# Graph network layer on one core: clearing ahead of every seventh gather, a fifth TensorE tile, one release per chunk

## The chip, the cores and the metric

The kernel runs on one core of a Trainium2 chip. The metric is the device time of one execution in microseconds, lower is better. TensorE (PE in the profile) multiplies matrices and writes PSUM; VectorE (DVE), ScalarE (ACT) and GpSimd (POOL) work on SBUF and PSUM; SyncE (SP) issues most DMAs. Each engine has its own instruction stream, and the streams meet only at semaphores.

## The reference

One layer of message passing over a graph of 6250 nodes with 64 features and 206,250 edges, sorted by destination (`dst`):

```python
h = jnp.maximum(_layernorm(x, axis=-1), 0.0)
msg = jax.nn.relu(h[src] + edge_attr)
agg = jax.ops.segment_sum(msg, dst, num_segments=x.shape[0])
z = jax.nn.relu((h + agg) @ W1 + b1)
out = x + (z @ W2 + b2)
```

## The kernel before, in words

The edges are cut into 124 chunks of 13 tiles with 128 edges each. Four chunks make a turn; there are 31 turns. Turn 0 is written out, turns 1 to 27 are a loop on every engine, and turns 28 to 30 (`EARLY_TURNS`) are written out again, since the two dense layers of the nodes that are already complete run beside them. Chunk number u of a turn has its own buffers (`gath[u]`, `onehot[u]`, `ends[u]`).

The rows `h[src]` of a chunk come in two ways. For most tiles GpSimd issues an indirect DMA per tile (`gather_rows`, L360), which fetches 128 rows of `h_table` from HBM. For the others TensorE picks the rows itself: `h` lies in SBUF as a high and a low float16 part (`table_hi`, `table_lo`); a one-hot of the source's block (`keyhot`) is multiplied with both, in seven blocks, so 14 matmuls of 448 columns per tile (`candidates`, L1083). The result holds seven candidate rows per edge in a PSUM bank of `ps_cand`; VectorE multiplies it with a mask (L842) and reduces it (L848) to the row that is wanted. `PE_TILES` says how many tiles of each chunk of a turn go this way: 4, 4, 4, 4, so that GpSimd gathers 9 per chunk.

VectorE adds the edge attributes to the gathered rows (L878, `sum_edges`), applies the ReLU and splits each partition's 13 edges by whether they belong to its first or its last destination (L888, `part_edges`, two instructions), reduces the parts over the 13 edges (L898, `add_parts`), and makes a one-hot of the destinations (L860). In the loop the edge attributes are copied by ScalarE into PSUM (L625, `edge_near`), and the sum and the parts read them there. TensorE multiplies `ends` with the one-hot (L384, `scatter_ends`), which adds the messages of a node up in a window of 64 nodes, and VectorE adds the window to `agg` (L919).

No planner sets the order; it is the order in which the code is written for each engine. Around the change these waits matter:

- GpSimd's gathers of chunk c wait for the chunk's indices, for the sum of the chunk four back (`summed`), which frees the buffer, and at four places in the chunk for TensorE to have finished one tile each of the chunk two back (`cands_ready`, the `released` argument, L358). The last kind protects no data; it sets the pace of the gathers.
- TensorE's tiles wait for a bank of `ps_cand` to be read (`masked`, four banks), and a chunk waits for its `keyhot`, two blocks of which VectorE makes and five ScalarE.
- VectorE's sum waits for the chunk's gathers (`gathered[u]`) and for its own last reduction.
- SyncE loads keys, indices and edges for two chunks at a time (`load_pair`).

## Time and profile before

| | us |
|---|---|
| three runs | 1792.00, 1792.09, 1795.76 (median 1792.09) |
| profiled execution, its own time | 1784.28 |
| its span | 1782.5 |
| TensorE busy | 1503.6 (84%) |
| VectorE busy | 1400.8 (79%) |
| GpSimd busy | 1107.6 (62%) |
| ScalarE busy | 793.4 (45%) |
| mean granted TensorE clock, share of full speed | 0.918 |

The span runs from the first to the last instruction; the rest of the execution's own time lies around it. Busy shares are averages over the start, the loop and the end. Matmuls are pipelined, so that the mean duration of one, as the page gives it, overlaps the next one. "issue" as a releaser means that an engine waited for nothing that the profile shows; "remote" is a releaser that the profile can't place.

### The profile page before, as it was taken

What the parts mean: (1) busy time and instruction counts of PE and PEld (TensorE: products, weight loads), DVE (VectorE), ACT (ScalarE), POOL (GpSimd) and SP (SyncE); (2) the same over time, 40 slices, a digit from 0 to 9 for tenths busy, and PEclk for the clock granted to TensorE, in tenths of its full rate; (3) what the DMA queues carried; (4) which work ended last, traced back from release to release, by engine and by line L of the source; (5) the groups of instructions that cost most, each with busy time, mean ns of one, the idle gap of its engine ahead of it and who ended that gap; (6) DMA issues with size and microseconds to landing.
All of it is one profiled execution on the core that took longest, in us unless ns stands there. A gap on an engine that the chain in (4) does not pass through costs nothing.

```text
span 1782.5 us, 26009 instructions
## 1 busy us (share of the span) xinstructions
PE 1503.6 (84%) x7987; PEld 729.3 (41%) x7987; DVE 1400.8 (79%) x2068; ACT 793.4 (45%) x883; POOL 1107.6 (62%) x1139
## 2 busy tenths in 40 slices
PE   5597898889888899888988888988889889898775
PEld 3243344434444444444434434434444444443432
DVE  8587788878887887878878878777888788798565
ACT  5244444544544544444445444544454445453321
POOL 5776566666666666656666666566666666567660
PEclk9798899999999999989989999989999999998896
DMA  4312122222222222221222222212222222222120
GB/s 165 94 45 73 46 73 72 48 72 72 47 73 71 47 73 53 67 72 47 72 67 52 72 57 63 71 47 73 72 47 73 68 51 73 66 53 73 45 60 20
DMA packets 67162, 115.15 MB, mean 65 GB/s; under 512 B 29810, under 2 KB 32882, under 8 KB 67010
## 3 DMA queue, kind: packets, MB, share of 16 engines
q1 hardware_dynamic: 30130, 75.86, 13.1%
q0 software_dynamic: 36000, 36.94, 11.3%
q10 hardware_dynamic: 1008, 2.06, 0.3%
q8 instruction: 12, 0.20, 0.0%
q14 instruction: 12, 0.10, 0.0%
HBM read 111.43 MB, written 3.34 MB: 64 GB/s over the span
## 4 chain that ended last, share of the span: by engine, by line
PE 77%; issue 13%; DVE 6%; POOL 1%; another core or an unknown queue 1%; DMA 0%; DVEq 0%; ACT 0%; ACTq 0%
PE ps_cand L1083 74%; PE ps L384 2%; DVE parts L888 2%; POOL gath L360 1%; DVE picked L842 1%; DVE gath L848 1%; PE ps_edge L413 1%; DVE ends L898 1%; PE ps_edge L428 1%; DMA xh<-x_rows 0%; DVE xh L751 0%; DVE row_ssq L742 0%; DVEq L909 0%; DVE side L796 0%
## 5 line engine op out<-in xcount | busy, mean ns | idle before, releaser
L360 POOL DMA_INDIRECT gath<-h_table,idx_pair x1125 | 1100.1, 978 | 629.3 <-issue 317.1
L1083 PE MATMUL ps_cand<-table_hi,keyhot 128*128 128x448 f16 x3388 | 1247.9, 368 | 80.6 <-issue 76.9
L1083 PE MATMUL ps_cand<-table_lo,keyhot 128*128 128x448 f16 x3388 | 1246.7, 368 | 69.8 <-issue 68.5
L1083 PEld LDWEIGHTS ps_cand<-table_hi,keyhot 128*128 128x128 f16 x3388 | 342.4, 101 | 450.4 <-issue 169.6
L842 DVE TENSOR_TENSOR picked<-ps_cand,cand_mask 128x448 f32<-128x448 f32 x487 | 300.8, 618 | 277.7 <-remote 170.4
L1083 PEld LDWEIGHTS ps_cand<-table_lo,keyhot 128*128 128x128 f16 x3388 | 342.3, 101 | 424.4 <-issue 151.4
L634 ACT ACTIVATE keyhot<-key_pair,key_bias 128x512 f16<-128x512 f16 (+2 forms) x600 | 375.4, 701 | 161.8 <-remote 93.0
L625 ACT ACTIVATE ps_edge<-edge_pair 128x832 f32<-128x832 f32 x108 | 93.7, 868 | 663.7 <-DVE parts L888 442.9
L888 DVE SCALAR_TENSOR_TENSOR parts<-ps_edge,side 128x832 f32<-128x832 f32 x216 | 326.2, 1587 | 1.7 <-issue 1.7
L848 DVE TENSOR_REDUCE gath<-picked 128x64 f32<-128x448 f32 x487 | 296.3, 608 | 4.1
L638 ACT ACTIVATE keyhot<-keyhot,hot_bias 128x2560 f16<-128x2560 f16 (+2 forms) x120 | 287.2, 2393 | 3.9
L898 DVE TENSOR_REDUCE ends<-parts 128x128 f32<-128x1664 f32 x124 | 232.4, 1874 | 0.0
L878 DVE TENSOR_TENSOR ps_edge<-gath,ps_edge 128x832 f32<-128x832 f32 x108 | 110.0, 1019 | 0.0
L384 PE MATMUL ps<-onehot,ends 128*32 128x64 f32 x992 | 49.4, 236 | 69.1 <-issue 68.1
L727 DVE TENSOR_SCALAR keyhot<-key_pair,key_iota 128x512 f16<-128x512 f16 (+2 forms) x268 | 82.4, 352 | 0.5 <-issue 0.3
L384 PEld LDWEIGHTS ps<-onehot,ends 128*32 128x32 f32 x992 | 26.8, 112 | 105.4 <-issue 104.2
L919 DVE TENSOR_TENSOR agg<-agg,ps 128x64 f32 x124 | 27.4, 221 | 53.1 <-DVE agg L919 25.9
L419 ACT ACTIVATE xh<-ps_edge,b_sb 64x448 f32<-64x448 f32 (+2 forms) x14 | 8.8, 628 | 106.3 <-PE ps_edge L413 91.3
L860 DVE TENSOR_TENSOR onehot<-iota_f,place 128x128 f32<-128x128 f32 x124 | 35.0, 282 | 20.8 <-remote 20.8
L413 PE MATMUL ps_edge<-agg,w_sb 128*64 128x448 f32 (+2 forms) x28 | 18.0, 738 | 36.6 <-DVE agg L919 13.9
L888 DVE SCALAR_TENSOR_TENSOR parts<-xh,side 128x832 f32<-128x832 f32 x32 | 48.4, 1591 | 0.0
L618 ACT ACTIVATE agg<-ps 64x512 f32<-64x512 f32 (+1 forms) x8 | 7.3, 995 | 38.5 <-remote 29.1
(77 smaller groups left out, 161.3 us busy)
## 6 DMA issues: line engine op xcount, KB each, us to landing
edge_pair<-edges_t SPq DMA_DIRECT2D x62, 832.0 KB
gath<-h_table,idx_pair POOLq DMA_INDIRECT x1125
key_pair<-key_table SPq DMA_DIRECT2D x62, 256.0 KB
h_table<-xh SPq DMA_DIRECT2D x7, 224.0 KB, 2.4
x_b<-x_cols SPq DMA_DIRECT2D x1, 1568.0 KB
out<-x_sq SPq DMA_DIRECT2D x6, 224.0 KB
idx_pair<-src_t SPq DMA_DIRECT2D x62, 13.0 KB
xh<-x_rows ACTq DMA_DIRECT2D x4, 224.0 KB, 5.0
```

The source lines that it names most:

```text
L360: nc.gpsimd.indirect_dma_start(out=gath[u][:, r, :], out_offset=None, in_=h_table, in_offset=bass.IndirectOffsetOnAxis(ap=idx[u][:, r:r + ...
L384: last = nc.tensor.matmul(bank[k * D + d:k * D + d + QUARTER, 0:WIN], ends[u][:, k, d:d + QUARTER], onehot[u][:, k, :], start=True, stop=True)
L625: nc.scalar.activation(edge_near, edge[u], ACT.Copy).then_inc(edge_copied, 1)
L634: last = nc.scalar.activation(keyhot[u % 2][:, a, 0:n], key[u][:, P * PE_MAX - n:], ACT.Abs, bias=key_bias[:, a:a + 1])
L638: nc.scalar.activation(keyhot[u % 2][:, DVE_BLOCKS:, 0:n], keyhot[u % 2][:, DVE_BLOCKS:, 0:n], ACT.Relu, bias=hot_bias[:, 0:1], scale=-1.0 ...
L727: last = nc.vector.tensor_scalar(keyhot[u % 2][:, a, 0:n], key[u][:, P * PE_MAX - n:], key_iota[:, a:a + 1], 1.0 / SCALE, ALU.is_equal, AL ...
L842: nc.vector.tensor_tensor(picked[i][:, :, :], ps_cand[buf][:, 0:D * CAND].rearrange("p (d b) -> p d b", b=CAND), mask.to_broadcast([P, D, ...
L848: nc.vector.tensor_reduce(gath[u][:, pool_tiles(t, u) + i, :], picked[i][:, :, :], AX_X, ALU.add).then_inc(selected, 1)
L878: nc.vector.tensor_tensor(edge_near if near(t) else edge_sum, gath[u][:, :, :], edge_near if near(t) else edge[u], ALU.add).then_inc(summe ...
L888: last = nc.vector.scalar_tensor_tensor(out=parts[:, k, :, :].rearrange("p d r -> p r d"), in0=edge_near if near(t) else edge_sum, scalar=0.0,
L898: nc.vector.tensor_reduce(ends[u][:, :, :], parts[:, :, :, :], AX_X, ALU.add).then_inc(ends_ready, 1)
L1083: last = nc.tensor.matmul(bank[:, 0:D * CAND], keyhot[u % 2][:, a, i * P:(i + 1) * P], half[:, a, :, :].rearrange("p d b -> p (d b)"), sta ...
```

## The change

- `rest` is new: GpSimd clears a scratch area of 128x832 float32 (`rest_area`), which nothing reads, ahead of every seventh gather in the loop. It waits for the clearing before it. In turn 0 and in the last three turns there is none.
- `PE_TILES` becomes 4, 5, 4, 4: in one chunk of a turn of the loop TensorE picks five tiles and GpSimd gathers eight. `place_bank` gives the 17 tiles of a turn their banks of `ps_cand`. Buffers of keys, masks and one-hots grow from 4 places to 5; turn 0 and the last three turns keep their tiles.
- `gather_chunk` waits for TensorE once per chunk, for the first tile of the chunk two back, in place of four times.
- SyncE loads the first two pairs of edges at the start, ahead of the key table's store and of `h_table`, in place of behind them.
- `scatter_ends` takes 64 columns of weights at once in place of two times 32.
- `part_edges` writes `parts` in order and reads the sums with a stride of 64 elements; before it read them in order and wrote with a stride.
- The input for the residual (`x_b`) is loaded in two pieces, behind the first and the second sum; the weights are loaded without a wait.

```diff
--- before.py
+++ after.py
...
@@ -57,6 +56,7 @@
 LAST_ROWS = 3
+X_PIECES = 2
 PARTS = [range(g * GROUP, (g + 1) * GROUP) for g in range(EARLY_GROUPS)] + \
...
@@ -73,16 +73,18 @@
-PE_TILES = (4, 4, 4, 4)
+PE_TILES = (4, 5, 4, 4)
 PE_FIRST = (3, 4, 4, 4)
 PE_LAST = ((4, 4, 4, 4), (3, 4, 3, 4), (3, 3, 2, 2))
 PE_MAX = max(PE_TILES)
 PE_TURN = sum(PE_TILES)
-assert PE_FIRST[-1] == PE_TILES[-1] and PE_MAX == max(*PE_FIRST, *PE_LAST[0], *PE_LAST[1], *PE_LAST[2])
+assert PE_FIRST[-1] == PE_TILES[-1] and PE_MAX >= max(*PE_FIRST, *PE_LAST[0], *PE_LAST[1], *PE_LAST[2])
 CAND = GROUP
 KEY_BLOCKS = N_GROUPS
 DVE_BLOCKS = 2
+REST_AFTER = 7
+REST_COLS = 832
 CAND_BANKS = 4
...
@@ -120,12 +122,17 @@
+def place_bank(place):
+    whole = PE_TURN // CAND_BANKS * CAND_BANKS
+    return place % CAND_BANKS if place < whole else (place - whole + CAND_BANKS // 2) % CAND_BANKS
+
+
 def cand_bank(t, u, i):
     if isinstance(t, int) and t == 0:
-        return (sum(PE_FIRST[:u]) + i + PE_TURN - sum(PE_FIRST)) % CAND_BANKS
+        return place_bank(sum(PE_FIRST[:u]) + i + PE_TURN - sum(PE_FIRST))
     if isinstance(t, int) and t in EARLY_TURNS:
         return (pe_before(t, u, i) - pe_before(EARLY_TURNS[0], 0)) % CAND_BANKS
-    return (sum(PE_TILES[:u]) + i) % CAND_BANKS
+    return place_bank(sum(PE_TILES[:u]) + i)
...
@@ -136,10 +143,10 @@
     place = sum(PE_TILES[:u]) + i
-    same = [q for q in range(place) if q % CAND_BANKS == place % CAND_BANKS]
+    same = [q for q in range(place) if place_bank(q) == place_bank(place)]
     if same:
         return pe_before(t, 0, same[-1] + 1)
-    return pe_before(t, 0, [q for q in range(PE_TURN) if q % CAND_BANKS == place % CAND_BANKS][-1] + 1 - PE_TURN)
+    return pe_before(t, 0, [q for q in range(PE_TURN) if place_bank(q) == place_bank(place)][-1] + 1 - PE_TURN)
...
@@ -351,12 +360,21 @@
-        def gather_rows(u, tiles, signal, released=None):
+        def rest(count):
+
+            if count is not None:
+                nc.gpsimd.wait_ge(rested, count)
+                nc.gpsimd.sem_inc(slot_taken, 1)
+            nc.gpsimd.memset(rest_area[:, :], 0.0).then_inc(rested, 1)
+
+        def gather_rows(u, tiles, signal, released=None, rests={}):
             for r in range(tiles):
-                if released is not None and r in released:
-                    nc.gpsimd.wait_ge(cands_ready, released[r])
+                if released is not None and r == 0:
+                    nc.gpsimd.wait_ge(cands_ready, released)
                     nc.gpsimd.sem_inc(slot_taken, 1)
+                if r in rests:
+                    rest(rests[r])
                 nc.gpsimd.indirect_dma_start(
...
@@ -380,9 +398,8 @@
             for k in range(ENDS):
-                for d in range(0, D, QUARTER):
-                    last = nc.tensor.matmul(bank[k * D + d:k * D + d + QUARTER, 0:WIN],
-                                            ends[u][:, k, d:d + QUARTER], onehot[u][:, k, :], start=True, stop=True)
+                last = nc.tensor.matmul(bank[k * D:(k + 1) * D, 0:WIN], ends[u][:, k, :], onehot[u][:, k, :],
+                                        start=True, stop=True)
             last.then_inc(signal, 1)
...
@@ -452,6 +469,9 @@
                 sp.dma_start(idx_pair[h][:, :, :], src_t[:, h * PAIR:(h + 1) * PAIR, :]).then_inc(idx_loaded[h], 16)
+            for h in range(PAIRS):
+                sp.dma_start(edge_pair[h][:, :, :, :], edges_t[:, h * PAIR:(h + 1) * PAIR, :, :]
+                             ).then_inc(edge_loaded[h], 16)
...
@@ -465,9 +485,6 @@
                              ).then_inc(h_stored, 16)
-            for h in range(PAIRS):
-                sp.dma_start(edge_pair[h][:, :, :, :], edges_t[:, h * PAIR:(h + 1) * PAIR, :, :]
-                             ).then_inc(edge_loaded[h], 16)
             def load_pair(t, h):
...
@@ -486,13 +503,15 @@
-            sp.wait_ge(summed, 1)
             sp.dma_start(b1_sb[:, :], b1).then_inc(weights_loaded, 16)
             for half in range(2):
                 sp.dma_start(w1_sb[half * D:(half + 1) * D, :], w1).then_inc(weights_loaded, 16)
             sp.dma_start(w2_sb[0:D, :], w2).then_inc(weights_loaded, 16)
             sp.dma_start(w2_sb[D:D + 1, :], b2).then_inc(weights_loaded, 16)
-            sp.dma_start(x_b[:, :, :], x_cols).then_inc(weights_loaded, 16)
+            for k in range(X_PIECES):
+                rows = slice(k * NODES_PER_PART // X_PIECES, (k + 1) * NODES_PER_PART // X_PIECES)
+                sp.wait_ge(summed, k + 1)
+                sp.dma_start(x_b[:, rows, :], x_cols[:, rows, :]).then_inc(weights_loaded, 16)
...
@@ -544,9 +563,13 @@
                 old_t, old_u = back(t, u, 2)
-                n, m = pool_tiles(t, u), pe_tiles(old_t, old_u)
-                gather_rows(u, n, gathered[u], {i * n // m: pe_before(old_t, old_u, i) + 1 for i in range(m)})
-
+                before = sum(pool_tiles(1, k) for k in range(u))
+                rests = {r: (before + r) // REST_AFTER for r in range(pool_tiles(1, u)) if (before + r) % REST_AFTER == 0}
+                turn_rests = sum(pool_tiles(1, k) for k in range(SLOTS)) // REST_AFTER
+                gather_rows(u, pool_tiles(t, u), gathered[u], pe_before(old_t, old_u) + 1,
+                            {} if isinstance(t, int) else {r: t * turn_rests + (n + 1 - turn_rests) for r, n in rests.items()})
+
+            pool.sem_inc(rested, 1)
             with pool.Fori(1, EARLY_TURNS[0]) as t:
...
@@ -886,10 +909,10 @@
                     last = nc.vector.scalar_tensor_tensor(
-                        out=parts[:, k, :, :].rearrange("p d r -> p r d"), in0=edge_near if near(t) else edge_sum,
+                        out=parts[:, k, :, :], in0=(edge_near if near(t) else edge_sum).rearrange("p r d -> p d r"),
                         scalar=0.0,
-                        in1=side[:, bass.ds(t * SLOTS + u, 1), k, :].rearrange("p c r -> p (c r)").unsqueeze(2)
-                        .to_broadcast([P, TILES_PER_CHUNK, D]), op0=ALU.max, op1=ALU.mult)
+                        in1=side[:, bass.ds(t * SLOTS + u, 1), k, :].rearrange("p c r -> p (c r)").unsqueeze(1)
+                        .to_broadcast([P, D, TILES_PER_CHUNK]), op0=ALU.max, op1=ALU.mult)
                 last.then_inc(parted, 1)
...
```

What moves on GpSimd, in the loop's body from its start (line 544, now 563, waits for indices; 358, now 374 and 366, are register work of waits; 360, now 378, is the gather). Before:

```order
14 L544 ISA
15 L358 ISA
16 L360 DMA gath<-h_table,idx_pair 128x64 x2
17 L358 REGISTER_ALU
18 L360 DMA gath<-h_table,idx_pair 128x64 x2
19 L358 REGISTER_ALU
20 L360 DMA gath<-h_table,idx_pair 128x64 x2
21 L358 REGISTER_ALU
22 L360 DMA gath<-h_table,idx_pair 128x64 x3
```

And of the changed kernel, the same place, the first chunk and the beginning of the second:

```order
14 L563 ISA
15 L374 ISA
16 L366 ISA
17 L368 MEMSET rest_area 128x832
18 L378 DMA gath<-h_table,idx_pair 128x64 x7
19 L366 REGISTER_ALU
20 L368 MEMSET rest_area 128x832
21 L378 DMA gath<-h_table,idx_pair 128x64 x2
22 L563 REGISTER_ALU
23 L374 REGISTER_ALU
24 L378 DMA gath<-h_table,idx_pair 128x64 x5
25 L366 REGISTER_ALU
```

The nine gathers of a chunk stood in four groups, each behind a wait for TensorE; now they stand in runs of seven across the chunks, with a clearing between the runs.

What moves on TensorE, at the two scatters that follow the second chunk of a turn (L384, now L401). Before:

```order
361 L384 MATMUL ps<-onehot,ends 32x64 [waits ends_ready,accumulated]
362 L384 MATMUL ps<-onehot,ends 32x64 x3
363 L1091 REGISTER_ALU
364 L384 MATMUL ps<-onehot,ends 32x64 [waits ends_ready,accumulated,onehot_ready]
365 L384 MATMUL ps<-onehot,ends 32x64 x3
```

And of the changed kernel:

```order
376 L401 MATMUL ps<-onehot,ends 64x64 [waits ends_ready,accumulated]
377 L401 MATMUL ps<-onehot,ends 64x64
378 L1114 REGISTER_ALU
379 L401 MATMUL ps<-onehot,ends 64x64 [waits ends_ready,accumulated,onehot_ready]
380 L401 MATMUL ps<-onehot,ends 64x64
```

The scatters stand at the same place with the same waits, 14 matmuls of the fifth tile later, and have half as many matmuls.

## Rows read from the trace of the kernel before

**Rows 1.** The page, parts 1 and 4: busy us, share, instructions; shares of the last chain
```profile
PE 1503.6 (84%) x7987; PEld 729.3 (41%) x7987; DVE 1400.8 (79%) x2068; ACT 793.4 (45%) x883; POOL 1107.6 (62%) x1139
PE 77%; issue 13%; DVE 6%; POOL 1%; another core or an unknown queue 1%; DMA 0%; DVEq 0%; ACT 0%; ACTq 0%
```

**Rows 2.** The page, part 5: groups of instructions; busy us, mean ns, idle before
```profile
L360 POOL DMA_INDIRECT gath<-h_table,idx_pair x1125 | 1100.1, 978 | 629.3 <-issue 317.1
L1083 PE MATMUL ps_cand<-table_hi,keyhot 128*128 128x448 f16 x3388 | 1247.9, 368 | 80.6 <-issue 76.9
L842 DVE TENSOR_TENSOR picked<-ps_cand,cand_mask 128x448 f32<-128x448 f32 x487 | 300.8, 618 | 277.7 <-remote 170.4
L848 DVE TENSOR_REDUCE gath<-picked 128x64 f32<-128x448 f32 x487 | 296.3, 608 | 4.1
L888 DVE SCALAR_TENSOR_TENSOR parts<-ps_edge,side 128x832 f32<-128x832 f32 x216 | 326.2, 1587 | 1.7 <-issue 1.7
L878 DVE TENSOR_TENSOR ps_edge<-gath,ps_edge 128x832 f32<-128x832 f32 x108 | 110.0, 1019 | 0.0
```

**Rows 3.** Timeline of VectorE: one-hots of chunks, and its wait between two of them
```profile
118.22 0.28 DVE L860 TENSOR_TENSOR onehot<-iota_f,place 128x128 f32<-128x128 f32 x1
901.72 0.29 DVE L860 TENSOR_TENSOR onehot<-iota_f,place 128x128 f32<-128x128 f32 x1 [6.96 <-remote]
919.18 0.62 DVE L842 TENSOR_TENSOR picked<-ps_cand,cand_mask 128x448 f32<-128x448 f32 x1 [2.38 <-PE ps_cand L1083]
927.13 0.28 DVE L860 TENSOR_TENSOR onehot<-iota_f,place 128x128 f32<-128x128 f32 x1
1592.95 0.28 DVE L860 TENSOR_TENSOR onehot<-iota_f,place 128x128 f32<-128x128 f32 x1
```

**Rows 4.** Windows: us, busy time of each engine (instructions), granted clock, DMA share, GB/s
```profile
578.00:589.00 11.00, 11.00 (x59) 5.56 (x57) 10.37 (x15) 6.39 (x7) 8.20 (x9) 1.00 0.20 46
589.00:593.30 4.30, 0.82 (x8) 0.39 (x7) 3.45 (x4) 0.87 (x1) 1.89 (x2) 0.94 0.11 23
1227.00:1248.00 21.00, 21.00 (x102) 10.43 (x101) 15.30 (x26) 11.04 (x12) 13.13 (x15) 0.90 0.28 76
62.00:100.00 38.00, 19.24 (x56) 5.09 (x57) 10.72 (x18) 7.80 (x9) 25.71 (x25) 0.55 0.16 34
150.00:1590.00 1440.00, 1260.68 (x6777) 613.34 (x6776) 1161.87 (x1690) 678.92 (x740) 902.20 (x952) 0.94 0.25 63
```

**Rows 5.** Timelines of GpSimd, then TensorE: start, us, instruction, idle before and releaser
```profile
589.09 0.94 POOL L360 DMA_INDIRECT gath<-h_table,idx_pair  x1 [0.46 <-issue]
590.34 0.95 POOL L360 DMA_INDIRECT gath<-h_table,idx_pair  x1 [0.30 <-issue]
617.01 0.94 POOL L360 DMA_INDIRECT gath<-h_table,idx_pair  x1 [1.17 <-remote]
156.66 0.31 PE L384 MATMUL ps<-onehot,ends 128*32 128x64 f32 x3 [0.71 <-issue]
1575.00 0.34 PE L384 MATMUL ps<-onehot,ends 128*32 128x64 f32 x5 [1.11 <-issue]
```

**Rows 6.** Waits, whole span: engine, line, releaser; us in total, times, longest
```profile
PEld ps_cand L1083 <- issue: 321.0, 661, 3.4
POOL gath L360 <- PE ps_cand L1083: 138.0, 84, 5.4
```

**Rows 7.** Groups by shape, GpSimd and VectorE
```profile
L526 POOL IOTA iota_p<- 128x1 int32 x1 | 0.1, 119 | 0.0
L525 POOL IOTA iota_i<- 128x128 int32 x1 | 0.2, 236 | 0.4 <-POOLq L1207 0.4
L399 POOL TENSOR_TENSOR xh<-xh,row_mean 128x448 f32<-128x448 f32 x7 | 6.9, 1013 | 4.7 <-ACT row_mean L579 4.7
L772 DVE SCALAR_TENSOR_TENSOR table_lo<-xh,table_hi 128x448 f16<-128x448 f32 x7 | 5.9, 934 | 0.0
```

**Rows 8.** Timeline of GpSimd: its first gather
```profile
22.79 6.09 POOL L360 DMA_INDIRECT gath<-h_table,idx_pair  x1 [10.03 <-DMA h_table<-xh]
```

9 lines of the change are left out of this document (5 added, 4 removed).

## The prediction

> **What bounds the kernel now.** I read the page's busy shares and its chain first. TensorE is busy for 84% of the span, and the chain that ended last runs through it for 77% and through "issue" for 13%, time in which an engine waited for nothing that the profile shows [rows 1]. So TensorE carries the end, and part of it is lost to something that isn't a semaphore. The costliest groups [rows 2] give the work of a turn of the loop. A turn is four chunks and takes 54.6 us: the one-hot of the first chunk of turn 1 starts at 118.22 and that of turn 28 at 1592.95, 27 turns later [rows 3].
>
> What each engine needs for a turn, if nothing waits:
> - TensorE: in a calm stretch 59 matmuls start in 11.00 us [rows 4], 0.186 us each. A tile has 14 of them, 2.61 us; 16 tiles are 41.8 us, with the scatters about 43.
> - VectorE: from the one-hot at 901.72 to the one two chunks later at 927.13 it waits once, 2.38 us [rows 3]. Two chunks are 25.41 - 2.38 = 23.0 us, a turn 46.1.
> - GpSimd: gathers that don't wait start 1.25 us apart (589.09 and 590.34), 0.94 of work and 0.30 behind it [rows 5]. 36 of them are 45.0 us.
>
> None reaches 54.6. The waits show where the rest is: the weight load stands idle for 321 us by "issue", 661 times [rows 6]. I walked through TensorE's and GpSimd's timelines from 150 to 1590 us and put together TensorE's idle spells of at least 0.4 us that lie under 3 us apart: 57 stretches, 139 spells, 150 us, the first spell ending at 156.66, the last at 1575.00 [rows 5]. Beside each I counted the gathers that GpSimd had issued without a pause. 54 of the 57 begin at the 8th to 11th gather of such a run, one at the 7th, and two right behind a run of nine and a pause of 1.17 us (the gather at 617.01 [rows 5]). None begins in a run of six or fewer. The windows show it from both sides [rows 4]: nine gathers and a full TensorE up to 589.00, then 0.82 us of matmuls in 4.30 us; 25 gathers without a pause and 19 of 38 us at a granted clock of 0.55 in the first turn; and in 1227 to 1248 fifteen gathers, broken by short pauses, with TensorE busy for 21.00 of 21.00 us. I can't name what TensorE lacks in a stretch; that long gather runs bring it on is as plain as a trace can make it.
>
> The price now: 150 us / 26.4 turns = 5.7 us of idle a turn. The clock falls from its upper to its lower level (2.4 to 1.2 GHz) behind such idle: 0.94 over 1440 us [rows 4] is 12% of the time at half speed, 173 us, of which half is lost, 3.3 us a turn. 43 + 5.7 + 3.3 = 52; the remaining 2.6 are short spells and waits on VectorE.
>
> One rule of the Trainium skill speaks against this reading. "Runtime: NRT & Kernel Launch", section Instruction fetch mechanics, puts fetch stalls at taken branches whose target isn't held, which no pause on GpSimd would touch. This case's trace doesn't agree: the stretch at 589 starts ahead of the loop's branch, and the one behind the gather at 617.01 [rows 5], half a turn later, lies in the middle of the body.
>
> **The change, part by part.** Times below are for a turn of the loop; 27 turns have the change, the first turn and the last three have no clearing.
> - A clearing of 128x832 float32 ahead of every seventh gather, five a turn. The trace has no such instruction. The nearest rows [rows 7]: an iota of one column 0.119 us and one of 128 columns 0.236, so 0.92 ns per further column and 0.88 us for 832; a subtraction with two inputs 1.013 us for 448, 2.26 ns per column, 1.88 us. Bounds: 0.12 us, if width costs nothing, and 1.9; I take 0.88, since the iota too only writes. With one more 0.30 us behind it a rest adds 1.18 us, five add 5.9.
> - 35 gathers in place of 36: 43.75 us. GpSimd's turn is 43.75 + 5.9 = 49.6 us (45.9 to 54.7 between the bounds).
> - A fifth tile on TensorE in one chunk: 14 x 0.186 = 2.6, so 44.4 and with the scatters, whose matmuls are half as many, about 45. VectorE gains a product (0.618) and a reduction (0.608) [rows 2] that overlap by a tenth: 46.1 + 1.2 = 47.3.
> - VectorE writes the parts in order and reads the sums with a stride, before the other way. Before: 1.587 us for 832 against 1.019 for the sum of the same size [rows 2], so the strided side costs 0.57. A strided read is in the trace only from SBUF: 0.934 for 448 columns [rows 7] against the 0.618 of VectorE's product of 448 in order [rows 2], 0.7 ns per column, which for 832 is again 0.57 to 0.59. So I take no gain. The lower bound, that a strided read of PSUM costs nothing, would give VectorE 8 x 0.57 = 4.5 us a turn. Either way VectorE (42.8 to 47.3) stays below GpSimd's 49.6, and the sum doesn't move.
> - One release per chunk in place of four. A release is a wait of GpSimd on TensorE; 138 us in 84 waits have TensorE as their last releaser [rows 6], and they are what breaks the gather runs now. If they go, nothing but the clearing breaks them. Behind the waiting instruction are the gathers of the chunk, and VectorE's sum waits for those. With GpSimd as the slowest engine the one wait left is mostly met when it is reached; I add 1.0 us a turn for it and for the waits on loaded indices.
> - Edges ahead of keys: two transfers of 832 KB are issued some 17 us earlier, ahead of the key table's. They are done before the first sum needs them now too; nothing gained, up to 2 us lost if the keys land later. The residual's input in two pieces, its second behind another sum: used only in the last turns, nothing. Wider masks and keys (5 places for 4) make the first turn's masks and key work about 2 us longer.
> - The last three turns keep their tiles, with one release for four and no clearing: runs of nine and more. They take stalls now and will then; I put nothing, with 8 us to either side.
>
> The rest decides whether the stretches go. A cycle is 7 gathers and a rest, 9.9 us, 1.42 us per gather. The stretch from 1227 to 1248 had 1.40 us per gather, broken as finely, and no stall [rows 4]. I take it that they go, and with them the low clock: TensorE then has 45 us of work in a turn of 50 and short idle spells only.
>
> Sum: a turn becomes 49.6 + 1.0 = 50.6 us, 4.0 less; 27 turns give -108; the start +2. The profiled execution took 1784.3 us by its own time (span 1782.5, 1.8 around it), so 1678; the runs' median, 1792.1, is 7.8 above that execution, so 1686.
>
> The skill has a price for the clearing that no row has: "GPSIMD Engine Reference", section 3.1, gives a one-input loop at best 769 ns for 512 elements. By it, as an estimate, the clearing is 1.25 us, GpSimd's turn 51.5, and the whole about 1737 - no run here shows it yet.
>
> **The rivals.**
> 1. Part of the stalls stays. The pause of 1.17 us at 617 did not stop the stretch behind a run of nine [rows 5], and 1.42 us per gather, kept up for a whole turn, is denser than the 54.6 / 36 = 1.52 of now. If half of the 9.0 us of stall and low clock stays, TensorE's turn is 45 + 4.5 + 2.6 = 52.1, 1784.3 - 67 + 10, about 1727; if the clearing costs 1.9 us as the subtraction would, GpSimd's 54.7 gives today's time, 1792. Range 1718 to 1792. Chance 0.19, of which 0.04 ends within 0.2% of now.
> 2. The clearing is cheap and enough. At its lower bound GpSimd needs 45.9, and VectorE's 47.3 is the bound (or TensorE's 45, if the parts get faster): 27 x 7.3 = 197 less, about 1597; with part of the waits kept, up to 1645. For it: nothing shows how little GpSimd must leave free. Against it: it takes a one-column price for 832. Chance 0.07.
> 3. Slower. GpSimd's clearing doesn't count as a pause: the stretches come as before, since what disturbs TensorE goes on while GpSimd is busy with anything, and the fewer releases lengthen the runs. Its place is TensorE's stream in the loop; its price is the fifth tile on a bound engine, 27 x 2.6 = 70, so 1862, and more if runs lengthen. It decides when the clearing saves less than 2.6 of the 9.0 us a turn. For it: every pause in the trace is idleness, none is work of GpSimd. A harsher form: the first gather behind other GpSimd work took 6.09 us [rows 8]; if every switch cost that, the turn would gain 26 us. Against that: it came once, and the gathers behind it took 0.94. Chance 0.14.
>
> **How the numbers follow.** Forecast (1645 to 1718): 0.60. A difference under 0.2%, some 3.6 us, can't be told from none. Faster: 0.60 + 0.15 + 0.07 = 0.82; same 0.04; slower 0.14. The range reaches from 1640, a little into rival 2, to 1790, through rival 1: outside are about 0.04 below and 0.14 above.
>
> **What would show it.** Right: the weight load's idle by "issue" falls from 321 us to under 120, what is left sits in the first turn and the last three; the granted clock from 150 us on is above 0.97; GpSimd has no wait over 1 us in the loop and a turn of 50 to 51; clearing near 0.9 us. VectorE's parts at 1.6 us (1.0 would say that PSUM's stride is free). Wrong: stretches of issue idle in the loop behind seven gathers and a clearing; gathers over 2 us behind a clearing; a turn at or above 54.6.

## The result and the profile after

The changed kernel takes 1891.95 us (1883.06 to 1896.21, 4 runs) beside 1793.24 for the kernel before (1792.0 to 1795.76): ratio 1.0535, 95% interval 1.0514 to 1.0557. It is 5.3% slower; 1686 was forecast.

The page of the profiled execution, its parts 1 and 4 as in [rows 1]: busy time and share of each engine, then the engines' shares of the chain that ended last.

```profile
PE 1516.7 (80%) x7869; PEld 758.4 (40%) x7869; DVE 1353.0 (72%) x2122; ACT 824.4 (44%) x883; POOL 1187.5 (63%) x1247
...
PE 67%; DVE 11%; another core or an unknown queue 11%; issue 9%; DVEq 1%; DMA 1%; ACTq 0%; ACT 0%
```

The chain goes less through TensorE and "issue" than before, and 11% of it now runs through a releaser that the profile can't place. Part 5 (busy us, mean ns, idle before and its releaser), to be read against [rows 2]:

```profile
L378 POOL DMA_INDIRECT gath<-h_table,idx_pair x1098 | 1071.4, 976 | 602.7 <-issue 297.4
L1106 PE MATMUL ps_cand<-table_hi,keyhot 128*128 128x448 f16 x3577 | 1306.3, 365 | 282.2 <-DVE picked L865 230.4
...
L865 DVE TENSOR_TENSOR picked<-ps_cand,cand_mask 128x448 f32<-128x448 f32 x514 | 317.2, 617 | 472.9 <-remote 330.8
...
L911 DVE SCALAR_TENSOR_TENSOR parts<-ps_edge,side 128x832 f32<-128x832 f32 x216 | 210.0, 1013 | 0.0
L368 POOL MEMSET rest_area<- 128x832 f32 x135 | 108.7, 805 | 50.2 <-PE ps_cand L1106 48.1
```

None of these instructions became slower, and the parts fell from 1587 to 1013 ns. (Those that make the wider keys of the fifth tile did, ScalarE's from 701 to 725 ns on the mean.) What grew is waiting: TensorE 80.6 to 282.2 us ahead of the matmuls with `table_hi` (150 to 295 us with those of `table_lo`), VectorE 277.7 to 472.9 ahead of its picks (the product at L865). The view of the waits (us in total, times, longest), against [rows 6]:

```profile
DVE picked L865 <- remote: 330.8, 82, 19.1
...
POOL gath L378 <- PE ps_cand L1106: 283.2, 61, 18.8
PEld ps_cand L1106 <- DVE picked L865: 241.4, 25, 15.4
PE ps_cand L1106 <- DVE picked L865: 230.4, 23, 14.9
PEld ps_cand L1106 <- issue: 166.6, 407, 13.6
...
POOL rest_area L368 <- PE ps_cand L1106: 48.1, 24, 2.1
```

And two more lines of the same view of the kernel before:

```profile
POOL gath L360 <- remote: 164.1, 64, 5.2
...
PE ps_cand L1083 <- DVE picked L842: 2.4, 4, 1.3
```

The weight load's idle by "issue" fell from 321.0 to 166.6 us, as hoped. GpSimd's waits by name of TensorE seem to double, from 138.0 to 283.2, but before, 164.1 us more of them stood under "remote". The releases are counted one by one below. TensorE's wait on a pick now comes 23 times with 10 us each, where before it came 4 times with 2.4 us in all. The loop's turn, from the one-hot of turn 1 to that of turn 28, as in [rows 3]:

```profile
123.35 0.28 DVE L883 TENSOR_TENSOR onehot<-iota_f,place 128x128 f32<-128x128 f32 x1
...
1693.07 0.28 DVE L883 TENSOR_TENSOR onehot<-iota_f,place 128x128 f32<-128x128 f32 x1
```

58.1 us in place of 54.6: 27 x 3.5 = 95 of the 110 us by which the span is longer (1892.2 against 1782.5). The rest is what lies ahead of turn 1 (+5) and the last three turns (+10). The window of [rows 4] shows the clock at 0.91 against 0.94:

```profile
150.00:1590.00 1440.00, 1207.19 (x6345) 606.24 (x6345) 1052.69 (x1652) 671.49 (x700) 922.76 (x992) 0.91 0.22 60
```

What happens in a turn, in the timelines of GpSimd, VectorE and TensorE (start, us, instruction, idle before and releaser):

```profile
957.13 0.96 POOL L378 DMA_INDIRECT gath<-h_table,idx_pair  x1 [0.30 <-issue]
...
957.62 0.35 PE L1106 MATMUL ps_cand<-table_lo,keyhot 128*128 128x448 f16 x1
...
958.09 0.81 POOL L368 MEMSET rest_area<- 128x832 f32 x1
...
959.06 1.07 POOL L378 DMA_INDIRECT gath<-h_table,idx_pair  x1 [0.17 <-issue]
...
960.27 0.35 PE L1106 MATMUL ps_cand<-table_lo,keyhot 128*128 128x448 f16 x1
...
962.83 0.61 DVE L871 TENSOR_REDUCE gath<-picked 128x64 f32<-128x448 f32 x1
...
966.87 0.94 POOL L378 DMA_INDIRECT gath<-h_table,idx_pair  x1 [0.30 <-issue]
967.80 0.82 POOL L368 MEMSET rest_area<- 128x832 f32 x1
968.78 0.95 POOL L378 DMA_INDIRECT gath<-h_table,idx_pair  x1 [0.17 <-issue]
969.84 0.62 DVE L865 TENSOR_TENSOR picked<-ps_cand,cand_mask 128x448 f32<-128x448 f32 x1 [6.40 <-remote]
...
970.52 0.55 PE L1106 MATMUL ps_cand<-table_hi,keyhot 128*128 128x448 f16 x1 [9.90 <-DVE picked L865]
```

The tile that the pick at 969.84 reads was finished by the matmul at 957.62, which ended at 957.97. VectorE was free from 963.44. The pick starts 6.4 us later, 2.0 us behind the end of a gather run (967.81), when a clearing has passed and the next gather is already at work. What was late is neither work nor an engine but TensorE's signal. TensorE meanwhile did one more tile, to 960.62, and then needed the bank that this pick frees: 9.9 us lost. GpSimd, a few gathers later, waits for TensorE in its turn. The three wait in a circle, and a pick over 5 us late comes 23 times from 160 to 1500 us, about once a turn.

GpSimd's own waits show the same without VectorE. I put beside each of its releases (the waits on TensorE's tiles) the end of the tile that it waits for, from 160 to 1450 us:

| kernel | releases | waits over 0.6 us | of them for a tile already done | their median |
|---|---|---|---|---|
| before | 378 | 103 | 100 | 2.6 us |
| changed | 89 | 67 | 44 | 2.1 us |

So also in the kernel before nearly every wait at a release is no wait for TensorE's work. The tile is done, GpSimd has stopped issuing gathers, and the signal arrives mostly 2 to 3 us after the last of them. Such pauses, four or so a turn, are when TensorE's signals catch up. In the changed kernel there are three a turn, and the 23 that aren't for a done tile are the far side of the circle: they end 0.79 us after a tile that TensorE finished late. One row of the 44:

```profile
948.69 0.79 POOL L368 MEMSET rest_area<- 128x832 f32 x1 [1.99 <-PE ps_cand L1106]
```

Added up, these waits give the turn. In the kernel before they cost GpSimd 9.1 us a turn beyond the usual 0.30 between gathers; with 36 x 1.25 = 45.0 of work that is 54.1 of the 54.6 measured. In the changed kernel they cost 10.4; with 47.1 of work (35 gathers and five clearings of 0.67, see the second sitting) that is 57.5 of 58.1. So three of four releases went, and none of the waiting did.

### The profile page after: what moved, and what is told of

Read it like the earlier page. It is cut to its first block, busy times and chain, and to the rows that moved or that the text cites. A ratio compares the mean times of both kernels' runs of the same rounds, so it can differ in the third digit from the quotient of the medians.

```text
span 1892.2 us, 25606 instructions
## 1 busy us (share of the span) xinstructions
PE 1516.7 (80%) x7869; PEld 758.4 (40%) x7869; DVE 1353.0 (72%) x2122; ACT 824.4 (44%) x883; POOL 1187.5 (63%) x1247
## 4 chain that ended last, share of the span: by engine, by line
PE 67%; DVE 11%; another core or an unknown queue 11%; issue 9%; DVEq 1%; DMA 1%; ACTq 0%; ACT 0%
PE ps_cand L1106 64%; DVE parts L911 3%; DVE picked L865 3%; DVE gath L871 3%; PE ps L401 1%; DVE ends L921 1%; PE ps_edge L430 1%; PE ps_cand L1080 1%; DVE keyhot L750 0%; DVEq L865 0%; PE ps_edge L445 0%; DMA xh<-x_rows 0%; DVE ps_edge L901 0%; DMA key_table<-key_h 0%
## 5 line engine op out<-in xcount | busy, mean ns | idle before, releaser
L1106 PE MATMUL ps_cand<-table_hi,keyhot 128*128 128x448 f16 x3577 | 1306.3, 365 | 282.2 <-DVE picked L865 230.4
L378 POOL DMA_INDIRECT gath<-h_table,idx_pair x1098 | 1071.4, 976 | 602.7 <-issue 297.4
L1106 PE MATMUL ps_cand<-table_lo,keyhot 128*128 128x448 f16 x3577 | 1302.0, 364 | 12.4 <-issue 12.2
L865 DVE TENSOR_TENSOR picked<-ps_cand,cand_mask 128x448 f32<-128x448 f32 x514 | 317.2, 617 | 472.9 <-remote 330.8
L1106 PEld LDWEIGHTS ps_cand<-table_hi,keyhot 128*128 128x128 f16 x3577 | 359.6, 101 | 652.5 <-DVE picked L865 241.4
L871 DVE TENSOR_REDUCE gath<-picked 128x64 f32<-128x448 f32 x514 | 314.5, 612 | 5.1
L911 DVE SCALAR_TENSOR_TENSOR parts<-ps_edge,side 128x832 f32<-128x832 f32 x216 | 210.0, 1013 | 0.0
L368 POOL MEMSET rest_area<- 128x832 f32 x135 | 108.7, 805 | 50.2 <-PE ps_cand L1106 48.1
L750 DVE TENSOR_SCALAR keyhot<-key_pair,key_iota 128x512 f16<-128x512 f16 (+3 forms) x268 | 107.0, 443 | 1.9 <-DMA key_pair<-key_table 1.5
L430 PE MATMUL ps_edge<-agg,w_sb 128*64 128x448 f32 (+2 forms) x28 | 19.5, 787 | 48.4 <-DVE x_sq L455 24.6
L911 DVE SCALAR_TENSOR_TENSOR parts<-xh,side 128x832 f32<-128x832 f32 x32 | 49.6, 1590 | 0.0
L401 PE MATMUL ps<-onehot,ends 128*64 128x64 f32 x496 | 31.3, 238 | 7.9 <-issue 6.8
L401 PEld LDWEIGHTS ps<-onehot,ends 128*64 128x64 f32 x496 | 21.4, 139 | 34.8 <-issue 33.7
```

Source lines behind the costliest of these rows:

```text
L368: nc.gpsimd.memset(rest_area[:, :], 0.0).then_inc(rested, 1)
L378: nc.gpsimd.indirect_dma_start(out=gath[u][:, r, :], out_offset=None, in_=h_table, in_offset=bass.IndirectOffsetOnAxis(ap=idx[u][:, r:r + ...
L750: last = nc.vector.tensor_scalar(keyhot[u % 2][:, a, 0:n], key[u][:, P * PE_MAX - n:], key_iota[:, a:a + 1], 1.0 / SCALE, ALU.is_equal, AL ...
L865: nc.vector.tensor_tensor(picked[i][:, :, :], ps_cand[buf][:, 0:D * CAND].rearrange("p (d b) -> p d b", b=CAND), mask.to_broadcast([P, D, ...
L871: nc.vector.tensor_reduce(gath[u][:, pool_tiles(t, u) + i, :], picked[i][:, :, :], AX_X, ALU.add).then_inc(selected, 1)
L911: last = nc.vector.scalar_tensor_tensor(out=parts[:, k, :, :], in0=(edge_near if near(t) else edge_sum).rearrange("p r d -> p d r"), scala ...
```

## The experiments

They ran in five sittings, each with the kernel before beside it on the same chip. The sittings differ so much that no number can be read without knowing which it is from: the kernel before took 1781.4, 1497.7, 1798.5, 1777.6 and 1499.4 us in them. Ratios below are always to the kernel before of the same sitting. I call the second and the fifth calm, the others, and the one of the prediction, disturbed. Third and fifth ran on a chip with the same number, so the difference needn't be one between chips.

| run | sitting | us | ratio (95% interval) |
|---|---|---|---|
| e1_four_releases | 1, disturbed | 1751.1 | 0.984 (0.979 to 0.990) |
| e2_no_clearing | 1 | 1816.1 | 1.021 (1.014 to 1.027) |
| e3_four_tiles | 1 | 1841.3 and 1849.1, its two fastest (median of four 1863.5) | 1.036 (of these two; no interval) |
| e4_one_release | 1 | 1857.1 | 1.046 (1.039 to 1.052) |
| e5_four_no_clearing | 2, calm | 1512.6 | 1.010 (1.008 to 1.012) |
| e6_parts_only | 2 | 1498.9 | 1.001 (1.000 to 1.002) |
| e7_two_clearings | 2 | 1686.9 | 1.126 (1.124 to 1.128) |
| e8_clearing_only | 2 | 1588.9 | 1.061 (1.060 to 1.063) |
| h1_changed_again | 3, disturbed | 1888.9 | 1.051 (1.047 to 1.055) |
| h2_four_no_clearing_again | 3 | 1762.2 | 0.980 (0.978 to 0.982) |
| h3_two_clearings_again | 3 | 1779.3 | 0.991 (0.987 to 0.995) |
| h4_one_release_again | 3 | 1836.5 | 1.020 (1.018 to 1.023) |
| g1_pause_per_chunk | 4, disturbed | 1852.6 | 1.042 (1.038 to 1.046) |
| g2_parts_only_again | 4 | 1777.3 | 1.001 (0.998 to 1.003) |
| g3_clearing_only_again | 4 | 1781.8 | 1.002 (1.000 to 1.005) |
| g4_clearing_1200 | 4 | 1823.8 | 1.028 (1.023 to 1.033) |
| k1_every_fourth | 5, calm | 1629.3 | 1.088 (1.086 to 1.089) |
| k2_every_fourth_four_releases | 5 | 1628.0 | 1.087 (1.085 to 1.089) |

### Undoing one part at a time (sitting 1)

e1_four_releases: the changed kernel, with the releases of before, one per tile of the chunk two back.

```diff
-                if released is not None and r == 0:
-                    nc.gpsimd.wait_ge(cands_ready, released)
+                if released is not None and r in released:
+                    nc.gpsimd.wait_ge(cands_ready, released[r])
...
-                gather_rows(u, pool_tiles(t, u), gathered[u], pe_before(old_t, old_u) + 1,
...
+                n, m = pool_tiles(t, u), pe_tiles(old_t, old_u)
+                gather_rows(u, n, gathered[u], {i * n // m: pe_before(old_t, old_u, i) + 1 for i in range(m)},
...
```

> The changed kernel with the release of before: GpSimd waits for TensorE once per tile of the chunk two back (four or five times a chunk), the clearing and the fifth tile stay. Theory 1, the single release is the cause: what TensorE sends and fetches gets through only when GpSimd is idle for some 2 us, and these waits make such pauses; then most of the 99 us come back, 1790 us or less, and the weight load's idle on VectorE (241 us) falls under 60. Theory 2, the fifth tile with its bank is the cause: within 15 us of the changed kernel's 1892. Theory 3, the clearing is the cause: also near 1892.

e2_no_clearing: the changed kernel without its clearings.

```diff
-                rests = {r: (before + r) // REST_AFTER for r in range(pool_tiles(1, u)) if (before + r) % REST_AFTER == 0}
+                rests = {r: (before + r) // REST_AFTER for r in range(pool_tiles(1, u)) if False}
```

> The changed kernel without any clearing; everything else as changed. Theory 1: the clearing lets something through once in ten us, so without it the runs grow and it gets slower still, 1900 to 2000 us. Theory 3, the clearing costs time on GpSimd (five times 0.98 us a turn, 132 us in all) and brings nothing: 1800 us or less. Theory 2: within 20 us of 1892.

e3_four_tiles: the changed kernel with four tiles in every chunk.

```diff
-PE_TILES = (4, 5, 4, 4)
+PE_TILES = (4, 4, 4, 4)
...
-                rests = {r: (before + r) // REST_AFTER for r in range(pool_tiles(1, u)) if (before + r) % REST_AFTER == 0}
+                rests = {r: (before + r) // REST_AFTER for r in range(pool_tiles(1, u)) if (before + r) % REST_AFTER == 0 and before + r < 35}
```

> The changed kernel with four tiles in every chunk, as before, and nine gathers; five clearings a turn stay (the last run of a turn has eight gathers). Theory 2: TensorE's wait at the turn's 17th tile, which stands two picks behind in its bank, is gone; 1790 us or less. Theory 1: the late semaphores stay, since runs are no shorter: 1860 us or more.

e4_one_release: the kernel before with one release a chunk.

```diff
-                gather_rows(u, n, gathered[u], {i * n // m: pe_before(old_t, old_u, i) + 1 for i in range(m)})
+                gather_rows(u, n, gathered[u], {0: pe_before(old_t, old_u) + 1})
```

> The kernel before with one release per chunk in place of four and no other edit. Theory 1: slower than before by 40 to 120 us, with longer gather runs than 11 and more time in which VectorE waits for a tile that TensorE had already finished. Theory 2 and 3: within 15 us of before (1793), or a little faster, since a wait is gone.

With four releases the changed kernel is faster than before, 0.984; the one release alone makes the kernel before 4.6% slower (2.0% in sitting 3). So without the one release there is no loss, and alone it makes one. In e1 GpSimd's waits at releases fall to 6.0 us a turn, and the circle of the changed kernel is all but gone:

```profile
PEld ps_cand L1107 <- issue: 248.7, 463, 7.4
...
PE ps_cand L1107 <- DVE picked L866: 34.4, 14, 4.9
```

The circle isn't how one release costs time by itself, though. In e4, which has four tiles a chunk, it is missing, and the kernel is slow all the same:

```profile
PE ps_cand L1083 <- DVE picked L842: 1.7, 3, 1.4
```

In e3, with four tiles too, TensorE waits for no pick at all and loses its time by "issue" in its stead (the weight load 395.8 us). What e4 shows is longer waits at the releases: 11.4 us a turn against 9.1 in the kernel before, in a turn of 56.8.

The clearing, under one release, is a loss: without it 1.021, with it 1.05. Theory 1 had e2 at 1900 to 2000 us, slower still, and failed there; theory 3's 1800 or less came nearer. By GpSimd's count e2 saves the clearings' 3.35 us a turn and waits 11.8 in place of 10.4, which leaves 55.6 us (55.5 measured). Undoing the fifth tile brings little (1.036 against 1.05, some 30 us), so rival 3's price for it, 70 us, is not what was paid.

### The single parts again, and the clearing twice (sitting 2, calm)

e5_four_no_clearing is e1 with no clearing; e6_parts_only the kernel before with the parts layout of the change; e8_clearing_only the kernel before with five clearings a turn. e7_two_clearings is the changed kernel with this `rest`:

```diff
+        rested_half = sem("rested_half")
...
+            nc.gpsimd.memset(rest_area[:, :], 0.0).then_inc(rested_half, 1)
+            nc.gpsimd.wait_ge(rested_half, count)
+            nc.gpsimd.sem_inc(slot_taken, 1)
             nc.gpsimd.memset(rest_area[:, :], 0.0).then_inc(rested, 1)
```

> The changed kernel with the four releases of before and no clearing; five tiles, parts layout and loading order stay. Theory P (what TensorE and its signals lack comes through in pauses of GpSimd, and the four releases make enough of them): with the releases back a clearing of 0.98 us buys nothing, since it is shorter than the pauses that the releases make, so its 4.9 us a turn come back in part: 1725 to 1750, not above the 1751 of the kernel with four releases and the clearing. Rival C (the clearing does help where the releases set the long pauses, by cutting the runs between them): 1765 to 1790, above that kernel by 15 us or more, with more of TensorE's idle by issue than its 249 us.

> The kernel before with the parts layout alone (parts written in order, the sums read from PSUM with a stride). The parts instruction in the loop falls from 1587 to about 1013 ns, 8 x 0.57 = 4.6 us of VectorE a turn. Theory P: VectorE's late picks are set by GpSimd's runs and not by VectorE's work, but part of the turn is bound by VectorE between them; 5 to 25 us gained, 1755 to 1776. Rival V (VectorE bounds the turn outside the stalls, as 46.1 us of work in 54.6 might mean): 27 x 3 us or more, under 1710. Rival N: nothing, 1775 to 1785.

> The changed kernel, one release a chunk, with every clearing done twice (2 x 0.805 us and their gaps, about 1.95 us of GpSimd without a gather ahead of every seventh). GpSimd needs 35 x 1.25 + 5 x 1.95 = 53.5 us a turn. Theory P (the length of the pause between gathers decides, some 2 us, whatever GpSimd does in it): TensorE's idle by issue falls under 120 us, the late picks end in the pauses and stay under 3 us, the turn is 54 to 57 us, 1780 to 1860, faster than the changed kernel's 1892. Rival I (only a GpSimd that does nothing lets the others through; work of its own counts as more of the same): each clearing adds to the wait of VectorE as the first did: 60 us a turn or more, above 1930.

> The kernel before with five clearings a turn alone (four releases, four tiles a chunk, 36 gathers, GpSimd 45 + 4.9 = 49.9 us a turn). Theory P: the pauses that count are those of the releases; the clearing shortens GpSimd's slack and gives 1775 to 1815 against the 1781 of before. Rival C (the clearing cuts the runs and stops stalls): 1700 to 1760, with TensorE's idle by issue under 250 us against 321.

None of the four answers what it was sent for, since in this sitting there was nothing to cure. In e6, nearly the kernel before, GpSimd issues without a break for the whole loop (none of its 1125 gathers but the first starts over 0.4 us behind the one before), and no release makes it wait over 0.6 us (0 of 446 from 160 to 1450 us). The waits of GpSimd and of the weight load, and a window (columns as in [rows 4]):

```profile
POOL gath L360 <- issue: 338.6, 1111, 0.3
...
PEld ps_cand L1083 <- DVE picked L842: 78.7, 188, 1.8
PEld ps_cand L1083 <- issue: 48.3, 97, 2.0
```

```profile
400.00:600.00 200.00, 195.27 (x1140) 96.84 (x1139) 177.12 (x286) 112.32 (x123) 151.25 (x161) 1.00 0.28 77
```

What the sitting gives instead is the sum of the work by itself, with no late signal in it. GpSimd's timeline in e8:

```profile
500.52 0.95 POOL L373 DMA_INDIRECT gath<-h_table,idx_pair  x1 [0.30 <-issue]
501.47 0.81 POOL L363 MEMSET rest_area<- 128x832 f32 x1
502.44 0.95 POOL L373 DMA_INDIRECT gath<-h_table,idx_pair  x1 [0.16 <-POOL rest_area L363]
```

A clearing makes two gathers start 1.92 us apart in place of 1.25, thus costs 0.67 (the 0.30 behind a gather goes); a pair makes it 2.85, thus 1.60.

| run | GpSimd by count | turn measured |
|---|---|---|
| e6 | 36 x 1.25 = 45.0 | 45.3 |
| e8 | 45.0 + 5 x 0.67 = 48.4 | 48.7 |
| e7 | 35 x 1.25 + 5 x 1.60 = 51.8 | 52.2 |
| e5 | 35 x 1.25 = 43.8 | 46.1 |

In e5 it is TensorE that never rests:

```profile
400.00:600.00 200.00, 200.00 (x1107) 103.26 (x1106) 180.90 (x287) 116.70 (x121) 148.92 (x159) 1.00 0.29 79
```

In the other three GpSimd's count gives the turn within 1%, and every clearing is paid in full.

### The same four, where signals are late (sitting 3)

h1 is the changed kernel once more, h2 is e5, h3 is e7, h4 is e4.

> The changed kernel once more, on whichever chip this call gets: the kernel before took 1781 us on one chip (the disturbed one, late picks of 157 us in the trace) and 1498 us on another (the calm one, none). Theory P: with TensorE's late signals gone, only work counts. On a chip like the calm one GpSimd's 35 x 1.25 + 5 x 0.98 = 48.6 us is then the longest turn, TensorE's 46 below it: 1498 + 27 x (48.7 - 45.3) = 1590, plus or minus 12, ratio 1.06, and no late pick. On one like the disturbed chip 1870 to 1900 with 200 us of late picks or more. Rival G (the loss of the change on the calm chip is smaller since four tiles more on TensorE spare GpSimd a gather): 1500 to 1560.

> The changed kernel with four releases and without the clearing, which took 1512.6 us on the calm chip (ratio 1.010). On a calm chip the same again. On a disturbed chip theory P (the releases' pauses let the signals through, the clearing is too short to): 1725 to 1750, at or below the 1751 of four releases with the clearing. Rival C (the clearing helps there): 1765 to 1790.

> The changed kernel with every clearing done twice, which took 1686.9 us on the calm chip (ratio 1.126). On a calm chip the same again. On a disturbed chip theory P (a pause of some 2 us between gathers lets TensorE's signals through, whatever GpSimd does in it): 1780 to 1860, late picks under 100 us, ratio under 1.05. Rival I (only a GpSimd that does nothing lets them through): above 1930, late picks over 300 us.

> The kernel before with one release a chunk alone, 1857 against 1781 us on the disturbed chip (ratio 1.046). Theory P: the release sets no work and protects no data, so on a calm chip, where there is nothing to let through, it changes nothing: ratio 0.998 to 1.003. Rival R (one release lets GpSimd run ahead and makes TensorE or VectorE wait for other things, on any chip): ratio 1.02 or more on the calm chip too. On a disturbed chip 1.04 to 1.05 again.

The third sitting was disturbed, and h1 repeats the result (1.051). h3 says most about how a pause works: twice the clearing, so more work for GpSimd (in the calm sitting the pairs cost 174 us over e5, which has none), and here the kernel is 110 us faster than with one. Waits of h3, and a late pick of it:

```profile
PEld ps_cand L1110 <- issue: 279.0, 471, 12.9
...
PEld ps_cand L1110 <- DVE picked L869: 37.8, 21, 4.2
```

```profile
976.54 0.94 POOL L382 DMA_INDIRECT gath<-h_table,idx_pair  x1 [0.30 <-issue]
977.49 0.81 POOL L369 MEMSET rest_area<- 128x832 f32 x1
978.45 0.79 POOL L372 MEMSET rest_area<- 128x832 f32 x1 [0.15 <-issue]
...
979.33 0.62 DVE L869 TENSOR_TENSOR picked<-ps_cand,cand_mask 128x448 f32<-128x448 f32 x1 [5.75 <-remote]
```

The pick starts 0.09 us after the second clearing ended and before the next gather, 1.84 us after the first clearing began. So signals get through while GpSimd works, if it issues no gather for some time, and rival I fails. Theory P is right on the time, and wrong on one number: late picks (a pick that starts at least 0.8 us after VectorE is free and its tile done, 160 to 1500 us) were to be under 100 us and are 243 in 96 picks, against 323 in 114 of h1. What the pairs took away are the long ones: over 5 us there are 6 with 33 us, against 23 with 170. At the releases GpSimd waits 1.7 us a turn, against 10.4 in h1. The weight load's idle by "issue" didn't fall; it is 279.0 us, and 150.1 in h1.

That a pause must last as long as the signal takes is not shown. In the changed kernel 79 of its 110 late picks start 1.7 to 3.3 us behind the beginning of a pause of over 0.5 us between gathers, where 20% of the time lies, and 27 of these pauses are lone clearings, 0.97 us long.

h4 gave 1.020 where 1.04 to 1.05 was expected. With e4's 1.046 it says how far one and the same kernel moves between two disturbed sittings, 0.025, though h1 repeated within 0.003. h2 took 1762.2 us, over the 1725 to 1750 that theory P gave and just under rival C's 1765. By ratios h2 and e1 (0.980 without the clearing, 0.984 with it) show no use of the clearing under four releases, but they are from different sittings.

### Length of the pause and length of the run (sittings 4 and 5)

g1_pause_per_chunk is h3 with the pair ahead of each chunk; g4_clearing_1200 the changed kernel with one longer clearing; k1_every_fourth with one short clearing ahead of every fourth gather, nine a turn; k2 is k1 with four releases. g2 is e6 and g3 is e8. The lines that differ most:

```diff
 g1 (beside the second clearing of h3)
-                rests = {r: (before + r) // REST_AFTER for r in range(pool_tiles(1, u)) if (before + r) % REST_AFTER == 0}
+                rests = {0: u}
...
 g4
-REST_COLS = 832
+REST_COLS = 1200
 k1, k2
-REST_AFTER = 7
+REST_AFTER = 4
...
```

> The changed kernel (one release) with the pair of clearings ahead of each chunk, four a turn in place of five, so that runs are nine and eight gathers long. On a calm chip GpSimd's turn is 35 x 1.25 + 4 x 1.6 = 50.2 us, 2.0 less than with five pairs (52.2 there): ratio 1.09. On a disturbed chip theory P (each pause of some 1.9 us lets all signals through; between them GpSimd can run nine): turn 52.5 to 54, 1725 to 1765, below the 1779 of five pairs. Rival L (what counts is the length of the run, and nine is past the 8th to 11th gather at which stalls begin): 1790 to 1840.

> The kernel before with the parts layout alone, ratio 1.001 on the calm chip, where GpSimd's 45.0 us bound the turn. On a disturbed chip theory P: the holds are set by GpSimd's runs, so 4.6 us less of VectorE a turn shorten them little: ratio 0.985 to 1.000. Rival V (VectorE bounds the turn between the holds): 0.96 or less.

> The kernel before with five clearings a turn alone, ratio 1.061 on the calm chip, where they lie on the bound engine. On a disturbed chip theory P: the four releases make the pauses that count, the clearing makes GpSimd reach them later: ratio 1.00 to 1.02. Rival C (the clearing cuts the runs and saves stalls): ratio under 0.98.

> The changed kernel (one release) with clearings of 1200 columns in place of 832: 1.16 us of work, a pause of 1.28 us between gathers where one clearing makes 0.93 and two make 1.87. Theory P with a length that is needed (the pause counts by its length): between the ratios 1.051 of one and 0.991 of two, 1.005 to 1.04. Rival S (what helps is the second start of an instruction or the 0.17 us between two clearings): 1.05 to 1.07, as one clearing or worse. On a calm chip both give about 1.05.

> The changed kernel (one release) with the short clearing ahead of every fourth gather, nine a turn: GpSimd needs 35 x 1.25 + 9 x 0.66 = 49.7 us a turn. If the length of the runs decides on a disturbed chip (stalls begin at the 8th gather or later of a run, and a short pause is enough to start the count again): turn 51 to 54, ratio 0.95 to 0.99. If the length of the pause decides (0.93 us lets too little through, however often): ratio 1.03 or more, late picks over 200 us. On a calm chip GpSimd's 49.7 gives ratio 1.08 either way.

> The same with the four releases of before. On a disturbed chip, if the length of the runs decides: 0.95 to 0.98, at or below the 0.984 of four releases with every seventh; if the length of the pause decides, the releases do the work and nine clearings cost some of it back: 0.985 to 1.01. On a calm chip 1.08.

g4 came out in theory P's range: 1115 ns of clearing, a longer pause, 1.028, between 1.051 for 805 ns and 0.991 for two. The order isn't shown, since g4 is from another sitting, and 0.023 is no more than e4 and h4 differ.

g1 went against my number (1852.6 us, ratio 1.042, not under 1765) and lies above rival L's 1790 to 1840 too; the trace offers another reason than the run's length. The pair now stands behind the release, and the release costs its own pause first:

```profile
715.06 0.94 POOL L382 DMA_INDIRECT gath<-h_table,idx_pair  x1 [0.31 <-issue]
718.02 0.79 POOL L369 MEMSET rest_area<- 128x832 f32 x1 [2.02 <-remote]
718.97 0.79 POOL L372 MEMSET rest_area<- 128x832 f32 x1 [0.15 <-POOL rest_area L369]
719.91 0.95 POOL L382 DMA_INDIRECT gath<-h_table,idx_pair  x1 [0.15 <-issue]
```

In 160 to 1450 us 67 of 91 releases wait, 52 of them for a tile already done, median 2.08 us, so that the pair comes where the signals have just arrived. All waits at releases in this stretch come to 7.0 us a turn, so by count GpSimd needs 35 x 1.25 + 4 x 1.60 + 7.0 = 57.2 us; 57.1 is measured. In h3 only 25 of 96 releases wait; there the pairs lie elsewhere, and the signals are mostly through when a release is reached. g1 doesn't tell the two reasons apart.

g2 and g3 are null results: neither the parts layout (1.001) nor five clearings (1.002) do anything to a kernel with four releases and late signals. In g3 the clearings' 3.35 us of work a turn are made up for by shorter waits at the releases, 5.7 us against 9.1.

k1 and k2 fell into a calm sitting, so whether short pauses do where runs are short stays open. They show one thing: 1629.3 and 1628.0 us with one and with four releases, a turn of 50.1 in both, against 43.75 + 9 x 0.67 = 49.8 by count. Where signals aren't late the number of releases makes no difference in this pair.

### What stays open

What the signals of TensorE are held up by isn't settled. In the disturbed traces the late signals come beside back-to-back gathers of GpSimd, and no run takes the gathers away. They don't suffice: in the calm sittings the same gathers (0.94 us each, 1.25 apart) run on for the whole loop with no late signal. Something outside the kernel adds to it; the instructions take the same time in both, apart from matmuls at a lower clock. One thing differs in the profile itself. The gathers' line among the DMA issues (its last number is the median us to landing) stands in e6, calm, and in g2, the same kernel disturbed, like this:

```profile
gath<-h_table,idx_pair POOLq DMA_INDIRECT x1125, 2.4
...
gath<-h_table,idx_pair POOLq DMA_INDIRECT x1125
```

g2 has no landing time, since most records of it are missing: 6005 completions of DMAs are recorded, against 21,199 in e6, and of TensorE's and VectorE's semaphore updates some are missing too. So a "remote" in a disturbed trace can be a lost record. The late starts are read from instructions and don't depend on it. But whether the recording of the profile has a part in the lateness no run tests.

The changed kernel itself was not run in a calm sitting. From the counts GpSimd would need 35 x 1.25 + 5 x 0.67 = 47.1 us a turn, 1.8 to 2.1 above the kernel before; that would be 1546 to 1555 us beside 1498, as an estimate, so slower there too.

No version that was run in both kinds of sitting beats the kernel before in both. h2 (four releases, no clearing, the rest of the change) has the lowest ratio where signals are late, 0.980; where they aren't, the kernel before has, and e5, the same kernel as h2, is 1% behind it.

## Why the prediction was wrong

The steps in their order:

- **What bounds the kernel.** Right that TensorE loses time beside its work and that GpSimd's unbroken runs go with it: the calm sittings put the price at 54.6 - 45.3 = 9.3 us a turn, and I had 9.0. That the two agree is partly luck: mine was TensorE's idle and clock over its own 43 us, the measured one is over GpSimd's 45. I read the loss in one place only, TensorE's idle by "issue". The other sign was in [rows 6] and [rows 2] and was taken for plain waiting: GpSimd's 138 us on TensorE, and VectorE's 170 us on "remote" ahead of picks. GpSimd's further 164 us on "remote" I left out. Most of these were waits for late signals.
- **The clearing.** 0.88 us was taken from the iotas of [rows 7]; it is 0.805. With the gap behind it, 1.18 was charged, and 0.67 is paid. Mis-sized on the safe side. The estimate from "GPSIMD Engine Reference", section 3.1 of the Trainium skill, was 1.25 us, from a loop of 769 ns for 512 elements; this case's clearing doesn't run like that loop, 0.805 us for 832 columns.
- **The parts layout.** No gain was taken; the instruction fell from 1587 to 1013 ns, the bound that I named (a strided read of PSUM is free; the same read from SBUF still takes 1590). Harmless: g2 and e6 show no change of the time (1.001 in both).
- **One release per chunk: the step that failed.** I wrote that the releases "are what breaks the gather runs now. If they go, nothing but the clearing breaks them", and then charged the one that is left 1.0 us a turn and let the clearing stand in for the other three. A release isn't a break of fixed length. It lasts until TensorE's signal is through, 2.6 us at the median where the kernel before waits. The clearing's break is 0.97 us, begins whether a signal is due or not, and didn't take those waits over. The term of 1.0 us a turn measures 10.4: the wait that was left is not "mostly met" but takes 2.1 us 44 times and more 23 times, 250 us from 160 to 1450 us. e1 against the changed kernel prices the three releases that went: 1.0535 - 0.984 = 0.07 of 1781, some 125 us, 4.6 a turn, over two sittings.
- **"I take it that they go."** The choice rested on gathers per microsecond, 1.42 against 1.40 in the calm stretch of [rows 4]. Density wasn't it: g3, with clearings as dense and all four releases beside them, still has 352 us of weight load idle by "issue". The one row that spoke of a break's length, the 1.17 us at 617.01 in [rows 5] that didn't stop a stretch, was named in rival 1 and given too little weight: it is longer than the clearing's 0.97.
- **The sum.** 49.6 us of work and 1.0 of waiting were put down for GpSimd; it has 47.1 of work and 10.4 of waiting in a turn of 58.1.
- **The rivals.** Rival 3 comes nearest with 1862, and its mechanism is half right. Right is that fewer releases hurt and that the clearing doesn't replace them. Wrong is the reason ("GpSimd is busy with anything"): in h3's pairs of clearings it is busy too, and they help. Wrong is its price, the fifth tile on a bound TensorE, 70 us: e3 without it is still at 1.036. That 1862 lies nearest to 1892 is luck.

By the forecast's own signs: issue idle 167 us (under 120 was asked), clock 0.91 (0.97), no wait of GpSimd above 1 us (up to 7.6 from 160 to 1450 us), a turn of 50 to 51 (58.1).

The rule that I set aside, "Runtime: NRT & Kernel Launch", Instruction fetch mechanics (the Trainium skill), puts fetch stalls at taken branches. The wait for the late pick of each turn in the changed kernel does begin 4 to 6 us behind VectorE's branch. But e5 has the same branches, and its trace has no late pick at all and 13.9 us of weight load idle by "issue" at ps_cand. The rule alone doesn't explain them.

## What to carry to other kernels

A wait that "protects no data" can still do work: before one is removed, look how long it lasts and whether what it waits for was already done when it began. If it was, the wait may be a pause that something else needs, and to remove it can move the waiting elsewhere and not end it. How long a pause must be to stand in for it these runs don't settle. And before tuning against a loss that no engine's work explains, time the unchanged kernel in several sittings: here it moved by 20% on its own, and most of what helped in one state cost time in the other.
